# Square roots and exponentials of the last two query groups, taken group by group instead of together

## The reference

```python
scores = -dist(q, k) / 4      # dist: distance of two tokens' 3 coordinates, pos = layernorm(x) @ w3d.T + b3d
scores = where(k after q, -inf, scores)
attn = softmax(scores)        # the same for all 16 heads
x = x + (attn @ (layernorm(x) @ wv.T + bv)) @ wo.T + bo
x = x + experts(layernorm(x)) # 2 of 8 experts chosen per token, and two shared ones
```

## Time and profile before

| | us |
|---|---|
| median of 3 runs | 607.44 |
| lowest, highest | 603.81, 608.32 |
| the profiled execution's own time | 603.74 |
| its span | 601.7 |
| PE busy | 545.9 |
| DVE busy | 434.1 |
| ACT busy | 327.7 |
| POOL busy | 273.8 |

### The profile page before, as it was taken

How to read it: one execution, slowest core, us unless ns; L and a number is a source line. 1 busy time by engine, 2 the same in 40 slices (tenths; PEclk the granted TensorE clock), 3 DMA queues, 4 the chain that set the end, 5 groups by cost and what they waited for, 6 DMA issues and landing times.

```text
span 601.7 us, 11532 instructions
## 1 busy us (share of the span) xinstructions
PE 545.9 (91%) x3482; PEld 475.1 (79%) x3482; DVE 434.1 (72%) x1163; ACT 327.7 (54%) x692; POOL 273.8 (46%) x582
## 2 busy tenths in 40 slices
PE   5799999899999889459999997999999999998984
PEld 4785899887789855358888886888888888887864
DVE  4989899689987465877777645766666666665796
ACT  3559996459998055225545322555555555554321
POOL 3257300444600051055667661677777777776000
PEclk9989999999999979859999998999999999999997
DMA  8999400000000085012222222233333333331995
GB/s 267 320 295 80 2 1 2 1 2 0 2 2 1 1 330 195 0 68 76 72 82 89 90 90 80 82 107 107 101 107 107 102 106 106 108 107 62 298 356 186
DMA packets 57130, 63.05 MB, mean 105 GB/s; under 512 B 14736, under 2 KB 50448, under 8 KB 57072
## 3 DMA queue, kind: packets, MB, share of 16 engines
q1 hardware_dynamic: 49216, 43.75, 26.8%
q0 software_dynamic: 6480, 17.90, 8.4%
q10 hardware_dynamic: 1376, 0.66, 0.5%
HBM read 30.64 MB, written 31.65 MB: 104 GB/s over the span
## 4 chain that ended last, share of the span: by engine, by line
PE 56%; DVE 6%; issue 1%; ACT 1%; POOL 0%; DVEq 0%; POOLq 0%
PE bank L1475 16%; PE bank L1477 16%; PE bank L1476 16%; PE bank L1598 3%; PE bank L1614 3%; PE bank L1483 1%; PE bank L1527 1%; DVE YG L1376 1%; DVE h_lo L1405 0%; DVE X L1386 0%; PE bank L1500 0%; DVE mv L1236 0%; DVE hf L1395 0%; DVE X L1368 0%; DVE XN L1239 0%
## 5 line engine op out<-in xcount | busy, mean ns | idle before, releaser
L1091 POOL DMA_INDIRECT slots_in<-X,slot x64 | 69.5, 1086 | 63.3 <-DVE slot L1352 31.1
L1127 POOL DMA_INDIRECT token_out<-YS,to_row x71 | 71.9, 1012 | 48.7 <-DVE back L1442 44.7
L829 PE MATMUL a_bank<-VO,E_hi 128*128 128x258 f32 x272 | 77.9, 286 | 3.8 <-DVE E_lo L652 3.8
L833 PE MATMUL a_bank<-VO,E_lo 128*128 128x258 f32 x272 | 76.9, 283 | 0.0
L831 PE MATMUL a_bank<-VO,E_hi 128*128 128x256 f32 x272 | 76.7, 282 | 0.0
L1431 DVE TENSOR_TENSOR hr<-bank,sr 128x256 f32<-128x256 f32 x71 | 30.2, 425 | 60.9 <-ACT sr L1198 60.9
L1475 PE MATMUL bank<-W_hi,XST_hi 128*128 x142 | 62.4, 440 | 0.5 <-DVE XST_lo L1447 0.5
L1198 ACT ACTIVATE sr<-bank 128x256 f32<-128x256 f32 x71 | 27.3, 385 | 64.5 <-PE bank L1477 62.8
L1477 PE MATMUL bank<-W_hi,XST_lo 128*128 x142 | 57.2, 403 | 0.0
L1172 ACT ACTIVATE h_hi<-hf 128x512 fp32r<-128x512 f32 x32 | 20.2, 632 | 66.9 <-DVE hf L1395 59.2
L1476 PE MATMUL bank<-W_lo,XST_hi 128*128 x142 | 56.6, 399 | 0.0
(11 more groups left out here) (247 smaller groups left out, 1656.6 us busy)
## 6 DMA issues: line engine op xcount, KB each, us to landing
XS<-slots_in SPq DMA_DIRECT2D x71, 131.0 KB
slots_in<-blank SPq DMA_DIRECT2D x7, 1179.0 KB, 15.6
YG<-token_out SPq DMA_DIRECT2D x16, 512.0 KB, 8.8
W_raw<-in_wT_dram SPq DMA_DIRECT2D x8, 768.0 KB, 13.1
X<-in_x_dram SPq DMA_DIRECT2D x8, 512.0 KB, 7.6
out_dram<-X SPq DMA_DIRECT2D x32, 128.0 KB, 2.8
token_out<-YS,to_row POOLq DMA_INDIRECT x71, 2.5
slots_in<-blank SPq DMA_DIRECT2D x1, 1048.0 KB, 15.1
```

Source lines behind the costliest of these rows:

```text
L829: pe.matmul(O_ps[Q % 2][j][:, 0:D + 2], E_hi[:, n % NE, cols], VO[:, kt, 0:D + 2], start=(kt == 0), stop=False)
L833: mm = pe.matmul(O_ps[Q % 2][j][:, 0:D + 2], E_lo[:, n % NE, cols], VO[:, kt, 0:D + 2], start=False, stop=(kt == qt))
L1091: pool.indirect_dma_start(out=xs, out_offset=bass.IndirectOffsetOnAxis(ap=slot[k][:, t:t + 1], axis=0), in_=X[:, t, :], in_offset=None).th ...
L1127: pool.indirect_dma_start(out=ys, out_offset=bass.IndirectOffsetOnAxis(ap=to_row[:, i:i + 1], axis=0), in_=YS[:, i % NYS, :], in_offset=No ...
```

## The change

`halves` gets a third entry: group 2 alone, then group 3 alone. Groups 0 and 1 stay together.

```diff
-        halves = [range(0, GB // 2), range(GB // 2, GB)]
+        halves = [range(0, GB // 2), range(GB // 2, GB - 1), range(GB - 1, GB)]
         sq_blocks = [(Q, kt) for half in halves for kt in range(GT * half[-1] + GT)
                      for Q in range(max(kt // GT, half[0]), half[-1] + 1)]
         N_HI_POOL = blocks.index((halves[1][0], 0))
```

## The result

| | before | changed |
|---|---|---|
| median us (first comparison, 4 runs each) | 607.88 | 614.09 |
| lowest, highest | 603.81, 609.46 | 613.47, 614.74 |
| ratio, 95% interval | | 1.0113 [1.0061, 1.0164] |
| ratio in a second comparison | | 1.0109 [1.0071, 1.0147] |
| profiled execution: its own time, span | 603.74, 601.7 | 614.74, 613.0 |

The change makes the kernel 1.1% slower, 6 to 7 us. The forecast was 614.1. Some executions of these kernels fall into a slower state; all ratios here leave them out.

The account below looks back on a forecast made before the run. PE, busy 91% of the span, was taken to bound the kernel. Losses of 3.9 us in the first batch and 2.7 in the second, 6.6 together, on the median of 607.44 gave 614.1 us, range 611.5 to 616.5.

Parts of the forecast that it names:

- Distances cost nothing: Ahead of ACT's roots: the same 80 matmuls and 40 copies in another order cost nothing, as ACT hides them.
- Roots of group 2 and 3: On ACT, from two equations (0.105 us per instruction, 0.83 ns per column): 5.7 and 7.8 us; 12 extra instructions cost 1.3.
- The early gain: Block 12's high part comes 6.6 us sooner, so PE starts block 15 at 79.45 instead of 80.35: 0.90 us gained.
- The pause: ACT's table loads and group 3's roots between the high parts of blocks 20 and 21: PE waits 1.4 us.
- The lead of eight buffers: ACT gets at most eight blocks ahead of PE; block 20's high part needs a buffer from block 12.
- DVE's queue: Finishes of group 2 behind block 24 delay low parts; PE waits 0.5 at 24, 0.6 at 25 and 26, 1.7 at 27.
- Sum: Block 27 starts later by 3.9 us in the first batch and 2.7 in the second, 6.6 us together.
- Everything is passed on: Between the batches and at the stage of the experts, no work takes up the shift: all 6.6 us carried.
- (1): Rival, chance 0.08: PE's eight full blocks cover ACT's pause, only the early gain of 2 x 0.9 stays, 605.6 us.
- (2): Rival, chance 0.07: PE waits only for ACT and DVE catches up; loss 1.0 us per batch, 609.4 us.
- (3): Rival, chance 0.06: the clock falls after PE's clustered waits; PE loses some 1.8 us per batch, 617.7 us.
- (4): Rival, chance 0.05: a table switch between busy stretches costs 1.28 us beyond its load, 2.6 later per batch, 619.2 us.

## Why the prediction was right

Point by point, expected and then measured:

- *Distances cost nothing.* Shown: with their new order alone and one switch, the loss is that of the 12 instructions, and from the first distance of the first batch to its first product all traces take 21.68 to 21.72 us, in either order.
- *Roots of group 2 and 3: 5.7 and 7.8 us.* 5.72 and 7.80, so the 12 more cost 1.23, not 1.3; in one row of 28 they cost 1.12, 0.093 each, where I had 0.105. Instructions in a merged row overlap by about 0.1 and the last one's end stands out once per row, which my two equations did not allow for.
- *The early gain, 0.9 per batch.* 1.0, block 0 to block 20: the gap at block 15 is gone in both batches. I had put it down to ACT being late; the version with all finishes later shows that it also needs DVE's finishes ahead of low part 15. And the early high parts stand further ahead of PE than the two to three blocks that I wrote: that of block 15 is made at 73.23, 7.7 us before PE starts the block. Neither enters the sum.
- *The pause: PE waits 1.4 at block 21.* 1.52. The high part of block 20 starts 1.71 us behind the start of block 12 (76.57 to 78.28), where I had put 1.70. From there to the high part of block 21 I had 11.54 and it took 11.59; the rest are hundredths on the way over DVE.
- *The lead of eight buffers decides.* Right on the side of fewer buffers (1.45 for one). On the side of more, ACT's own queue takes over after 0.97, a second bound close behind the first that I had not worked out.
- *DVE's queue: 0.5 at 24, 0.6 at 25 and 26, 1.7 at 27.* 0.47, 0.48, 0.50, 1.55. The run with later finishes shows the terms at 25 to 27; the gap at 24 stays there and belongs to ACT's pause. Each gap is some 0.1 less because a product that starts after a wait takes 0.1 longer by its starts, which I had counted with the gap.
- *Sum: 3.9 and 2.7.* 3.95 and 2.81 in the trace, 6.2 us by the medians, 6.9 by the ratio.
- *Everything is passed on.* Nothing was taken up: the stretch between the batches is 44.15 us before and 44.15 in the run with later finishes, whose first batch ends later. It did vary by 2.6 us, but without the change too.
- *Rivals.* The pause was not covered (1), PE did not wait for ACT alone (2), the granted clock stayed 1.00 from 84 to 112 us through all five gaps and from 184 to 208 through those of the second batch (3), and a switch cost no more than 1.35 (4).

The forecast of 614.1 against 614.09 is closer than the method deserves: the runs of the old kernel spread over nearly 6 us in the first comparison, and the median on which the sum was put could have lain 2 us off.

## What to carry to other kernels

When a stage is cut into pieces so that its first results come sooner, look at what now stands between two pieces on the engine that does them. That pause must fit into the lead which the buffers behind it allow; add it up from rows, from the event that frees the last buffer to the next result. And an engine that has lost its lead pays again for work queued ahead of what is urgent: here the finishes queued in the way cost 4.3 us up to block 27 and the pause itself, the gaps at 21 and 24, 4.0 in two batches. Moving them by four blocks helped both the changed kernel and the one before.

## What the runs showed of the hardware

- The clock of TensorE between the batches fell in one execution and not in another of the same kernel, after the same 2 us of idle time: 0.61 or 1.00 from 116 to 120 us. With this dip and a second from 128 to 136 us the stretch took 2.5 us longer. Five gaps of up to 1.5 us in 12 us did not bring it down, nor did one of 2.96 us with seven buffers: PE was busy 0.58 of the 3 us from 92 to 95, and the granted clock was 1.00 there and up to 108. What decides stays open.
- Exchanging the function table costs 1.28 us and 0.02 to 0.1 around it. A copy over the same columns takes the same time as a square root, 7.79 and 7.80 us for 16.
- Leaving PE waiting makes the first block after it about 0.1 us longer by its starts: block 25 takes 1.54 us instead of 1.44 (starts at 95.79, its last query tile at 96.97, and that tile's pitch is 0.36).
